# A graph layer's edge counting: ScalarE makes four of fifteen destination one-hots, and the row transposes move into the second chunk

## The reference

```python
msg = x[src]
agg = jax.ops.segment_sum(msg, dst, num_segments=n)
deg = jax.ops.segment_sum(jnp.ones((src.shape[0],), x.dtype), dst, num_segments=n)
mean = agg / jnp.maximum(deg, 1.0)[:, None]
h = mean @ W_l + b + x @ W_r
return h * jax.nn.sigmoid(h)
```

## Time and profile before

| | us |
|---|---|
| median of 3 runs | 2565.68 |
| lowest and highest | 2557.02, 2566.22 |
| the profiled execution's own time | 2557.94 |
| its span | 2556.1 |
| TensorE busy | 2400.7 (94%) |
| VectorE busy | 1779.6 (70%) |
| ScalarE busy | 921.0 (36%) |
| GpSimd busy | 1641.0 (64%) |
| the counting stage: first matmul to last count | 19.64 to 154.42 |

### The profile page before, as it was taken

How to read it: one execution, slowest core, us unless ns; L and a number is a source line. 1 busy time by engine, 2 the same in 40 slices (tenths; PEclk the granted TensorE clock), 3 DMA queues, 4 the chain that set the end, 5 groups by cost and what they waited for, 6 DMA issues and landing times.

```text
span 2556.1 us, 34212 instructions
## 1 busy us (share of the span) xinstructions
PE 2400.7 (94%) x11520; PEld 2002.0 (78%) x11520; DVE 1779.6 (70%) x2626; ACT 921.0 (36%) x1124; POOL 1641.0 (64%) x721
## 2 busy tenths in 40 slices
PE   6989978888898779999999999999999999999999
PEld 6879776777897667777777777777777777777777
DVE  8983336658886587777777777777777777777775
ACT  3741236523886622222222222222222222222221
POOL 0023423238888747777777777777777777777773
PEclk9998979989998879999999999999999999999999
DMA  3024110023432102122221212121222212121211
GB/s 78 16 66 154 34 67 16 1 76 79 107 93 69 57 33 99 66 98 75 89 92 72 98 66 98 66 98 69 95 85 79 98 66 98 66 98 66 98 66 37
DMA packets 49887, 190.87 MB, mean 75 GB/s; under 512 B 13300, under 2 KB 17911, under 8 KB 33444
## 3 DMA queue, kind: packets, MB, share of 16 engines
q1 hardware_dynamic: 35728, 177.90, 19.9%
q0 software_dynamic: 13200, 10.75, 2.0%
q10 hardware_dynamic: 900, 1.44, 0.2%
HBM read 177.54 MB, written 12.35 MB: 74 GB/s over the span
## 4 chain that ended last, share of the span: by engine, by line
PE 82%; DVE 9%; POOL 4%; issue 2%; ACT 1%; DMA 1%; SPq 0%; DVEq 0%; ACTq 0%; POOLq 0%
PE PS L1612 25%; PE PS L1614 24%; PE PS L1613 24%; POOL gatW L741 2%; PE PS L1875 2%; PE PS L1690 2%; PE PS L1876 2%; DVE hotS L1103 1%; DVE hotD L1104 1%; DVE negmax L1321 1%; POOL XN L741 1%; DMA fil<-filters 1%; DVE XTl L1076 0%; DVE XN L1067 0%; PE PS L1754 0%
## 5 line engine op out<-in xcount | busy, mean ns | idle before, releaser
L1562 DVE SCALAR_TENSOR_TENSOR XN<-PS,attn,XN 125x512 f32<-125x512 f32 x1083 | 805.7, 749 | 441.2 <-PE PS L1614 432.5
L771 POOL TENSOR_TENSOR OPl<-TS,OPh 128x1024 fp32r<-128x1024 f32 x256 | 676.7, 2644 | 117.4 <-ACT OPh L1013 117.4
L771 POOL TENSOR_TENSOR OPl<-RAW,OPh 128x1024 fp32r<-128x1024 f32 x192 | 554.8, 2889 | 275.0 <-ACT OPh L1013 274.9
L1612 PE MATMUL PS<-OPh,XTh 128*125 128x512 f32 x1280 | 507.3, 396 | 2.0 <-DVE attn L1516 2.0
L1614 PE MATMUL PS<-OPh,XTl 128*125 128x512 f32 x1280 | 505.9, 395 | 0.0
L1613 PE MATMUL PS<-OPl,XTh 128*125 128x512 f32 x1280 | 503.5, 393 | 0.0
L1013 ACT ACTIVATE OPh<-TS 128x1024 fp32r<-128x1024 f32 x256 | 271.8, 1062 | 529.0 <-PE PS L1614 519.1
L1013 ACT ACTIVATE OPh<-RAW 128x1024 fp32r<-128x1024 f32 x192 | 203.9, 1062 | 581.3 <-PE PS L1614 581.3
L1612 PE MATMUL PS<-OPh,Sh 128*125 128x512 f32 x1024 | 404.8, 395 | 3.7 <-DVE XN L1559 3.7
L1614 PE MATMUL PS<-OPh,Sl 128*125 128x512 f32 x1024 | 404.1, 395 | 0.0
L1613 PE MATMUL PS<-OPl,Sh 128*125 128x512 f32 x1024 | 402.6, 393 | 0.0
(11 more groups left out here) (314 smaller groups left out, 3352.2 us busy)
## 6 DMA issues: line engine op xcount, KB each, us to landing
RAW<-in_values SPq DMA_DIRECT2D x64, 2048.0 KB, 7.5
filters<-filt SPq DMA_DIRECT2D x14, 672.0 KB
fil<-filters SPq DMA_DIRECT2D x11, 840.0 KB
Wraw<-in_ffn SPq DMA_DIRECT2D x4, 1024.0 KB, 5.6
Wraw<-in_L_q SPq DMA_DIRECT2D x2, 1024.0 KB, 5.0
Wraw<-in_L_k SPq DMA_DIRECT2D x2, 1024.0 KB, 7.5
Wraw<-in_L_v SPq DMA_DIRECT2D x2, 1024.0 KB, 7.0
gatW<-nodes,dstI POOLq DMA_INDIRECT x90, 3.6
```

Source lines behind the costliest of these rows:

```text
L771: g.tensor_tensor(OPl[:, j], operand_source(j, parity), OPh[:, j].bitcast(F32), ALU.subtract).then_inc(op_lower, 1)
L1562: v.scalar_tensor_tensor(out=XN[:, t], in0=PS[0:P, bank, :], scalar=w, in1=XN[:, t], op0=ALU.mult, op1=ALU.add).then_inc(v_added, 1)
L1612: mm(dst, lh, rh, start=start, stop=False, skip_group_check=resumed)
```

## The change

HOT_A = 4: of the 15 hotD of a chunk, ScalarE makes the last four, in two steps each. It writes |j - dstMod| into the buffer `away` (Abs), and then Relu(weight - weight * away) as hotD, which is the weight where the distance is 0, and 0 elsewhere. VectorE makes minusMod and minusWeight for that. TensorE waits for both semaphores, hot_ready and hot_a.

The start is put in another order. VectorE makes the one-hots of chunks 0 and 1 ahead of XN, with the statistics between. TensorE counts chunk 0 first, and each tile's transposes stand behind one sum of chunk 1. The five transposed tiles now all use PSUM slot 3. VectorE takes their rests between the one-hots of chunk 2.

```diff
@@ -120,7 +121,7 @@
-SLOT = {u: n % 4 for n, u in enumerate(UNITS)}
+SLOT = {u: 3 if u[0] == "xt0" else n % 4 for n, u in enumerate(UNITS)}
...
@@ -804,9 +814,26 @@
+            def act_one_hots(c):
+
+                if c >= 2:
+                    act.wait_ge(counted, T * (c - 1))
+                if c >= 1:
+                    act.wait_ge(hot_a, HOT_A * c)
+                for i in range(HOT_A):
+                    t = c * CH + CH - HOT_A + i
+                    a.activation(away[:, i], iota16[:, 0:HALF + 1], ACT.Abs, bias=minusMod[:, t:t + 1]).then_inc(away_ready, 1)
+                for i in range(HOT_A):
+                    t = c * CH + CH - HOT_A + i
+                    act.wait_ge(away_ready, HOT_A * c + i + 1)
+                    a.activation(hotD[:, c % 2, CH - HOT_A + i, :], away[:, i], ACT.Relu, bias=dstWeight[:, t:t + 1],
+                                 scale=minusWeight[:, t:t + 1]).then_inc(hot_a, 1)
+
             act.wait_ge(consts_ready, 2)
+            act.wait_ge(signs_ready, 1)
+            act_one_hots(0)
+            act_one_hots(1)
             layer_std(0)
-            transposed_upper("xt0")
...
             for c in range(NCH):
                 m = c // COUNT_CHUNKS
+                if 1 <= c < NCH - 1:
+                    act_one_hots(c + 1)
+                if c == 1:
+                    transposed_upper("xt0")
...
@@ -1096,11 +1131,15 @@
+            v.tensor_scalar(minusMod[:], dstMod[:], -1.0, None, ALU.mult)
+            v.tensor_scalar(minusWeight[:], dstWeight[:], -1.0, None, ALU.mult).then_inc(signs_ready, 1)
             dve.wait_ge(consts_ready, 2)
 
             def one_hot(c, parity, u):
                 t = c * CH + u
-                v.tensor_scalar(hotS[:, parity, u, :], iota16[:, 0:N + 1], srcF[:, bass.ds(t, 1)], None, ALU.is_equal)
+                ins = v.tensor_scalar(hotS[:, parity, u, :], iota16[:, 0:N + 1], srcF[:, bass.ds(t, 1)], None, ALU.is_equal)
+                if u >= CH - HOT_A:
+                    return ins
...
@@ -1109,17 +1148,21 @@
-            layer_norm(0, statistics(None, range(T)))
-            transposed_rest("xt0")
+            variances(statistics(None, range(T)))
+            for u in range(CH):
+                ins = one_hot(1, 1, u)
+            ins.then_inc(hot_ready, 1)
+            layer_norm(0)
...
-                if c < NCH - 1:
-                    if c > 0:
-                        dve.wait_ge(counted, T * c)
+                if 1 <= c < NCH - 1:
+                    dve.wait_ge(counted, T * c)
                     for u in range(CH):
                         ins = one_hot(c + 1, (c + 1) % 2, u)
+                        if c == 1 and u % 3 == 1:
+                            transposed_rest("xt0", (u // 3,))
...
@@ -1666,8 +1709,6 @@
-            transposes("xt0", 0)
-            wait_drained(pe, ("xt0", T - 1))
...
                 pe.wait_ge(hot_ready, c + 1)
+                pe.wait_ge(hot_a, HOT_A * (c + 1))
...
                     ins.then_inc(counted, 1)
+                    if c == 1:
+                        transposes("xt0", 0, tiles=(s,))
                 if c == F_FIRST:
+                    wait_drained(pe, ("xt0", T - 1))
                     pe.wait_ge(f_consts, F_CONSTS)
```

More of the change, by code:

```diff
@@ L27 @@
 COUNT_BANKS = 6
+HOT_A = 4
 F_FIRST = 1
@@ L218, in build @@
         for i in (1, 0):
-            Wraw[i], Wh[i], Wl[i] = sb(f"Wraw{i}", [128, K, D], F32), sb(f"Wh{i}", [128, K, D], F32R), sb(f"Wl{i}", [128, K, D], F32R)
+            Wraw[i], Wh[i] = sb(f"Wraw{i}", [128, K, D], F32), sb(f"Wh{i}", [128, K, D], F32R)
+            if i == 0:
+                with ExitStack() as s:
+                    away = sb("away", [P, HOT_A, HALF + 1], F32, s)
+                    minusMod = sb("minusMod", [P, ET], F32, s)
+                    minusWeight = sb("minusWeight", [P, ET], F32, s)
+            Wl[i] = sb(f"Wl{i}", [128, K, D], F32R)
         rows = sb("rows", [P, 4, D], F32)
@@ L377, in build @@
         hot_ready = sem("hot_ready")
+        signs_ready = sem("signs_ready")
+        away_ready = sem("away_ready")
+        hot_a = sem("hot_a")
         counted = sem("counted")
@@ L1057, in statistics, with variances @@
                 return ins
-            def layer_norm(n, last):
+            def variances(last):
                 link(last)
@@ L1063, in layer_norm @@
                 ins.then_inc(var_ready, 1)
+            def layer_norm(n, last=None):
+                if last is not None:
+                    variances(last)
                 dve.wait_ge(std_ready, n + 1)
@@ L1076, in rest, with transposed_rest @@
                 v.tensor_tensor(dst, value, upper_part.bitcast(F32), ALU.subtract).then_inc(drained_v, units)
-            def transposed_rest(stage):
-                for j in range(T):
+            def transposed_rest(stage, tiles=range(T)):
+                for j in tiles:
                     u = (stage, j)
@@ L1617, in finish, with transposes @@
                 ins.then_inc(filled, 1)
-            def transposes(stage, xn_count, src=XN, interleaved=False):
-                for j in range(T):
+            def transposes(stage, xn_count, src=XN, interleaved=False, tiles=range(T)):
+                for j in tiles:
                     u = (stage, j)
```

## The result

| | before | changed |
|---|---|---|
| median of 19 runs, us | 2566.22 | 2581.72 |
| lowest and highest | 2555.76, 2573.13 | 2567.92, 2587.77 |
| span of the profiled execution | 2556.1 | 2578.0 |
| last count ends | 154.42 | 171.80 |
| filter products behind it start | 164.10 | 179.55 |

The ratio is 1.006, with a 95% interval of 1.0049 to 1.0072: slower, by 15.5 us of the medians. The forecast was +15, or 2580 us, with a range of 2569 to 2588.

The account below looks back on a forecast made before the run. TensorE was busy 94% of the span; VectorE's work set the counting stage's 25.24 us ring with ScalarE. Chunk 9 late 13.0, clock 2.4 and tail 0 summed to +15 us, so 2580 us on the median, range 2569 to 2588.

Parts of the forecast that it names:

- The ring: Counting stage: ScalarE's cycle with VectorE over two chunks would take 30.6 us, against 25.24 before; chance 0.58.
- A: One ScalarE group of four Abs and four Relu: 4.04 us, or 3.68 at the lower bound.
- F: Odd chunks, from ScalarE's first field copy to its next softplus, including waiting for VectorE's hidden rows: 7.82 us.
- S: ScalarE's softplus without a hold: 7.34 us.
- The second operand of the Relu: ScalarE's Relu with bias and scale from memory: 0.55 us taken, 0.46 if the second is free.
- The start: Counting up to chunk 2: the new order would start chunk 2 at 41.8 instead of 47.9, winning 6.1 us.
- Set 1: VectorE's one-hots for chunk 1, whose end releases that chunk on TensorE: forecast to last until 23.8 us.
- Chunk 0's clock: TensorE's first count at half clock, shifting all some 2 us; part of a +20 to +23 rival, chance 0.10.
- Chunk 9: TensorE's chunk 9 would start at 147.0, 13.0 us late, with 2.4 us more for a fallen clock.
- The tail: From the count's end to the filter products: 1.6 us won, some 2 lost to the clock, net 0.
- cheaper: Counting stage: same ring, second operand free and clock held in chunk 9: +10, 2576 us; chance 0.28.
- the other side: Counting stage: ScalarE hides its groups, TensorE sets the pace, count ends 9.2 us sooner, 2556 us; chance 0.04.

Follow-up runs that it names:

- e3: The changed kernel with two one-hots of 15 on ScalarE instead of four; ratio to before 1.0006.
- e8: The changed kernel with VectorE adding the pair of hidden rows ahead of the fields instead of behind them; ratio to before 1.0021.
- e4: The changed kernel with ScalarE's one-hot groups of odd chunks moved behind the five fields, two chunks ahead of their use; ratio to before 1.0017.
- e7: The changed kernel with 34 identity matmuls ahead of chunk 0 and GpSimd's five factor instructions held until chunk 2's hot set is done; ratio to before 1.0062.
- e6: The changed kernel with unread identity matmuls in three TensorE waits: 34 ahead of chunk 0, 20 ahead of chunk 9, 18 in the tail; ratio to before 1.0030.
- e5: The changed kernel with ScalarE one-hots only for chunks 0, 1 and odd chunks, the latter from 3 on made behind the fields; ratio to before 0.9972.
- e12: e11 with 36 identity matmuls ahead of chunk 0, GpSimd's factor instructions later and ScalarE's Wh in step 8; ratio to before 0.9991.
- e11: e1 with VectorE adding the pair of hidden rows ahead of the fields, no one-hot on ScalarE; ratio to before 0.9984.
- e1: The changed kernel with its new start kept and all 15 hotD given back to VectorE; ratio to before 0.9990.
- e9: e5 with 34 identity matmuls ahead of chunk 0 and GpSimd's five factor instructions held until chunk 2's hot set is done; ratio to before 0.9970.
- e10: e9 with ScalarE's copy Wh moved from step 9 to step 8; median 2552.80 us, ratio to before 0.9968.

## Why the prediction was right, point by point

**The ring.** Forecast 2A + F + 2S = 30.6 us, measured 30.38. A was 3.95 (I took 4.04), F 7.82 and S 7.34 as read. Three runs show the terms: e3 (A halved) turns in 26.4 us, e8 (F cut to 4.99) in 27.5, and e4 (one group moved) in 27.9. The second operand of the Relu was not free: 0.54 us from one to the next, against 0.45 for the Abs.

**The start.** Chunk 0 at 13.12 (12.8), chunk 2 at 43.34 (41.8), chunk 3 at 57.95 (55.2), chunk 5 at 87.84 (85.8). So the 6.1 us that I counted as won were 4.6. Three terms were mis-sized. Set 1 was ready at 25.9 instead of 23.8, since GpSimd's factor instructions stood in VectorE's way (1.9 of the 2.1 us by the rows under e7). The transposes of a tile took 0.42 us instead of 0.87, which gave 2 us back. And chunk 2 ran at the lower clock, 12.83 us instead of 10.2, behind the wait of 1.68 us for the last rest, where I had looked for no such thing. That chunk moved the ring: ScalarE's softplus behind it waited for TensorE's filter layer, where I had it wait for nothing, and chunk 3 did not wait for ScalarE, as I had expected it to:

```profile
57.22 0.67 ACT L848 ACTIVATE soft<-PS,b1c 96x500 f32<-96x500 f32 x1 [1.30 <-PE PS L1721]
```

The waits ahead of chunks 5, 7 and 9 were 5.61, 3.68 and 5.35 us, not 6 to 8: the slow chunks filled part of the time that I had counted as waiting, which costs nothing while ScalarE sets the pace.

**Chunk 0's clock.** It took 12.57 us, not 10.2. I gave this a part of a 0.10 chance and wrote that the trace speaks against it, because the first 20 transposes took 4.35 us. That step failed: the transposes of the changed kernel and of e7, with TensorE long at work, are 0.42 us for four matmuls, so 20 of them are 2.1 us and before's had been at half pace all along. The Trainium skill, page "TensorE: Matmul & The Clock Gate", part 1, says that the throttled state is the default and that activity releases it. Chunk 0 agrees: 12.57 us as the first work, and in e6 10.34 behind 34 other matmuls. It cost little of the time, since chunk 1 waited for VectorE anyway (0.27 us ahead of it).

**Chunk 9.** 148.60 against 147.0 forecast, and 2.74 us for the clock against 2.4 (e6 takes them away). Count's end: +17.4 us, I had +15.4.

**The tail.** GpSimd's Wl took 4.53 us and the filter products came 7.75 us behind the count's end, where I had 4.6 and 8.1. The clock then fell, as I had feared: 0.50 from 179.5 to 184. That made +15.5 us at 179.55 and +17.9 by VectorE's last row of the mean (242.02 before, 259.92 now). So the tail as a whole was +0.5 us, where I had 0.

**The sum.** The profiled spans differ by 21.9 us, 4 more than this stage explains. They arise between 750 and 900 us (17.8 us at ScalarE's row of msgh at 732.74, 21.8 at its table load at 879.87), in work that the change doesn't touch. From the Wh of the next stage that waits for its weights (265.62 us in the changed kernel) to the span's end the fourteen profiled kernels take between 2301.6 and 2314.6 us, and faster or slower counting does not sort them. So one pair of spans tells little of a few microseconds here. The medians differ by 15.5. That the forecast of +15 met them within a microsecond is partly luck: the row-level loss is 2 to 3 us larger.

**The rivals.** The ring came as forecast and not cheaper. On the other side (ScalarE hides its groups, TensorE alone sets the pace) I had a count's end at 145.2. e5 comes there with half the groups, and elsewhere: its 148.6 is that sum with chunk 2 at 43.1 instead of 41.8, and 2.1 us slower.

## What to carry to other kernels

Work that is moved to a less busy engine costs nothing only where it stands in that engine's idle time; count the turn of the ring, with every wait in it, and not the engine's share. Here two groups that lengthen the ring cost 5 us a turn, and one group in the hold behind the fields won 1 us a turn. A gain at the start stays only if the bound behind it is the engine that gained. To call an engine full, look at a whole turn of its loop.

## What the runs showed of the hardware

- A granted clock of 1.00 in the stretch did not mean full pace at the kernel's first matmuls: 17 in 4.9 us, against 60 in 8.2 later. With 34 earlier matmuls chunk 0 took 10.34 us instead of 12.57.
- The clock's fall behind a wait does not go by its length alone. Behind 2.79 us ahead of chunk 9 before kept it and took 20.46 us for two chunks, and e12 took 22.03. Behind 0.97 us ahead of chunk 7 e12 took 10.33 us and e11 11.98. Behind the same 1.68 us chunk 2 took 12.83 us in the changed kernel and 10.34 in e7 and e11. There is one trace of each kernel, and what decides it was not settled.
- GpSimd's Wl lasted 4.53 us where it started in a pause of VectorE (the change). Where it started beside a working VectorE it lasted 4.83 (e1), 10.0 to 10.1 (before, e5, e9, e11), 11.42 (e12) and 13.75 us (e10). In all seven it ended 4.35 to 4.39 us behind the start of VectorE's first pause, and VectorE's next instruction lasted 4.2 to 4.3 us instead of 0.47.
